# A table-lookup and interaction kernel: the first table's ids sent to all partitions by DMA, the selection columns read with a step of zero

## What is computed

```python
e = jnp.stack([tbl_0[ids[:, 0]], tbl_1[ids[:, 1]], ..., tbl_26[ids[:, 26]]], axis=1)   # (512, 27, 128)
z = dot products of all pairs of rows of one sample, the lower triangle                # (512, 351)
h = jnp.concatenate([z, dense_ctx], axis=1)
h = jnp.maximum(h @ W_top1 + b_top1, 0.0)
h = jnp.maximum(h @ W_top2 + b_top2, 0.0)
y = h @ W_top3
```

## Time and profile before

| what | value |
|---|---|
| median of 3 runs | 109.08 us (108.71 to 110.86) |
| span of the profiled execution | 123.6 us |
| TensorE busy | 106.3 us, 86% |
| VectorE busy | 70.0 us, 57% |
| ScalarE busy | 67.2 us, 54% |
| GpSimd busy | 68.1 us, 55% |
| moved from memory | 12.06 MB, of it 7.75 MB in table and weight loads, 4.07 MB in gathers |
| chain that ended last | TensorE 68%, VectorE 16%, issue 13%, ScalarE 1% |

### The profile page before, as it was taken

How to read it: one execution, slowest core, us unless ns; L and a number is a source line. 1 busy time by engine, 2 the same in 40 slices (tenths; PEclk the granted TensorE clock), 3 DMA queues, 4 the chain that set the end, 5 groups by cost and what they waited for, 6 DMA issues and landing times.

```text
span 123.6 us, 3473 instructions
## 1 busy us (share of the span) xinstructions
PE 106.3 (86%) x1496; PEld 86.1 (70%) x1496; DVE 70.0 (57%) x98; ACT 67.2 (54%) x112; POOL 68.1 (55%) x71
## 2 busy tenths in 40 slices
PE   6998799899999899999329993789458999997992
PEld 6534487687887687788219883669448999797891
DVE  6799999999999999999900050015001060103401
ACT  4596929899999999995200052025301144531442
POOL 3777888888888888887744166416560665000000
PEclk9999999999999999999985599558975699999999
DMA  3896366966984574711210101110200011000000
GB/s 79 262 237 190 101 204 146 293 198 155 302 235 111 172 229 108 205 48 42 54 52 17 31 29 42 27 48 21 66 24 27 21 48 41 23 5 5 5 0 1
DMA packets 5305, 12.06 MB, mean 98 GB/s; under 512 B 1765, under 2 KB 2277, under 8 KB 5290
## 3 DMA queue, kind: packets, MB, share of 16 engines
q1 hardware_dynamic: 3282, 7.75, 22.0%
q0 software_dynamic: 1984, 4.07, 12.8%
q10 hardware_dynamic: 24, 0.02, 0.1%
HBM read 11.83 MB, written 0.00 MB: 96 GB/s over the span
## 4 chain that ended last, share of the span: by engine, by line
PE 68%; DVE 16%; issue 13%; ACT 1%; DVEq 0%
PE ring L512 21%; PE gram_ps L539 12%; DVE marks L651 10%; PE gram_ps L512 8%; PE ring L592 5%; PE ids_ps L574 4%; PE ring L523 4%; DVE low L628 3%; PE ids_ps L567 2%; PE ids_ps L523 2%; PE ring L574 2%; PE ring L602 2%; PE ids_ps L592 1%; DVE pick L610 1%; PE ids_ps L553 1%
## 5 line engine op out<-in xcount | busy, mean ns | idle before, releaser
L422 POOL DMA_INDIRECT rows<-tbl,ids_sb x62 | 67.1, 1082 | 36.3 <-issue 15.9
L651 DVE TENSOR_TENSOR marks<-ids_ps,row_no 125x1024 fp32r<-125x1024 f32 (+2 forms) x39 | 43.5, 1148 | 0.0
L512 PE MATMUL ring<-marks,high 125*128 125x512 f32 (+1 forms) x64 | 26.6, 416 | 1.7 <-issue 1.6
L539 PE MATMUL gram_ps<-rowsT 128*27 128x27 f32 x1024 | 15.8, 206 | 11.4 <-issue 11.2
L512 PE MATMUL ring<-marks,low 125*128 125x512 f32 (+1 forms) x64 | 25.2, 394 | 0.0
L539 PEld LDWEIGHTS gram_ps<-rowsT 128*27 128x27 f32 x1024 | 13.3, 118 | 14.7 <-issue 14.0
L512 PEld LDWEIGHTS ring<-marks,high 125*128 125x128 f32 x64 | 12.8, 200 | 7.1 <-issue 4.6
L724 ACT ACTIVATE away<-ids_ps,row_no 125x512 f32<-125x512 f32 (+1 forms) x22 | 14.0, 715 | 4.7 <-PE ids_ps L466 4.1
L628 DVE TENSOR_TENSOR low<-raw,high 125x512 fp32r<-125x512 f32 (+1 forms) x23 | 16.2, 705 | 0.0
L672 DVE STREAM_TRANSPOSE gram<-gram_ps 128x416 f32<-128x416 f32 (+1 forms) x8 | 4.6, 612 | 18.1 <-PE gram_ps L539 18.1
L512 PEld LDWEIGHTS ring<-marks,low 125*128 125x128 f32 x64 | 12.9, 202 | 1.6
(11 more groups left out here) (61 smaller groups left out, 116.5 us busy)
## 6 DMA issues: line engine op xcount, KB each, us to landing
raw<-tbl SPq DMA_DIRECT2D x9, 448.0 KB
raw<-tbl SPq DMA_DIRECT2D x2, 560.0 KB
rows<-tbl,ids_sb POOLq DMA_INDIRECT x62
w_sb<-w SPq DMA_DIRECT2D x2, 256.0 KB
w_sb<-w SPq DMA_DIRECT2D x1, 512.0 KB
raw<-tbl SPq DMA_DIRECT2D x9, 52.0 KB
raw<-tbl SPq DMA_DIRECT2D x2, 224.0 KB
w_sb<-w SPq DMA_DIRECT2D x1, 192.0 KB
```

The source lines that it names most:

```text
L422: nc.gpsimd.indirect_dma_start(out=rows[0:n, i % ROW_BUFS, s, :], out_offset=None, in_=tables[PLACES[s]], in_offset=bass.IndirectOffsetOnA ...
L512: last = nc.tensor.matmul(bank[:, 0:n], part[:, i % SPLIT_BUFS, c * D:(c + 1) * D], mark_of(unit, c), start=c == 0 and part is high, stop= ...
L539: last = nc.tensor.matmul(gram_ps[s * STRIP:s * STRIP + F, g, 0:F], places, places, start=True, stop=True)
L651: nc.vector.tensor_tensor(marks_of(unit)[:, c0 - c1:, :], index.to_broadcast([TP, c1 - c0, n]), which.to_broadcast([TP, c1 - c0, n]), ALU. ...
```

## The change

The ids of job 0 no longer come over TensorE. A DMA on ScalarE's queue writes them to a new tile `first_ids` on all 128 partitions (the same 2 KB row read 128 times), and VectorE compares them there, still as integers, with a compare of one tensor against a per-partition scalar, 512 marks at a time: eight instructions for the four units. The cast of all ids to floats moves behind the first unit. TensorE's first three spreads are those of jobs 1, 2 and 3 instead of 0, 1 and 2, and there is none left in `find 0 1`. `pick` shrinks to one column per job, the first twelve columns of the identity, and the spread reads that column 128 times with a step of zero, so the two copies that wrote the blocks are gone. ScalarE makes `high` of job 1 ahead of its mark of job 1 instead of behind the distances of job 2.

```diff
-        pick = sb("pick", [P, len(FOUND), P], F32R)
+        pick = sb("pick", [P, len(FOUND)], F32R)
+        first_ids = sb("first_ids", [P, B], I32)
...
             def spread_ids(j):
                 b0, n = JOBS[j]
-                if j >= IDS_BANKS:
+                if j - IDS_BANKS >= 1:
                     pe.wait_ge(marked, through(BY_DVE, j - IDS_BANKS))
-                if j - IDS_BANKS >= 1:
                     pe.wait_ge(away_ready, j - IDS_BANKS)
-                if j == IDS_BANKS:
-                    pe.wait_ge(pick_ready, 2)
-                nc.tensor.matmul(ids_ps[:, j % IDS_BANKS, 0:n], pick[:, j, :], fids_r[:, b0:b0 + n],
+                nc.tensor.matmul(ids_ps[:, j % IDS_BANKS, 0:n], pick[:, j:j + 1].to_broadcast([P, P]), fids_r[:, b0:b0 + n],
                                  start=True, stop=True).then_inc(spread, 1)
...
-            for j in range(IDS_BANKS):
+            for j in range(1, IDS_BANKS + 1):
                 spread_ids(j)
...
-                        if c1 == CHUNKS[i] and i + IDS_BANKS < len(JOBS):
+                        if c1 == CHUNKS[i] and i >= 1 and i + IDS_BANKS < len(JOBS):
                             spread_ids(i + IDS_BANKS)
...
             dve.wait_ge(ident_ready, 1)
-            pick_for(0, IDS_BANKS)
-            dve.wait_ge(fids_cleared, 1)
-            dve.wait_ge(fids_in, 16)
-            nc.vector.tensor_copy(fids_r[0:len(FOUND), :], fids[:, :]).then_inc(fids_ready, 1)
+            nc.vector.tensor_copy(pick[:, :], ident[:, 0:len(FOUND)]).then_inc(pick_ready, 1)
...
+            def ids_ready():
+                dve.wait_ge(fids_cleared, 1)
+                dve.wait_ge(fids_in, 16)
+                nc.vector.tensor_copy(fids_r[0:len(FOUND), :], fids[:, :]).then_inc(fids_ready, 1)
...
-                if c0 == 0:
-                    dve.wait_ge(spread, j + 1)
-                    if j >= 1:
-                        dve.wait_ge(away_ready, j)
+                if u == 0:
+                    dve.wait_ge(first_ids_in, 16)
+                elif c0 == 0:
+                    dve.wait_ge(spread, j)
+                    dve.wait_ge(away_ready, j)
...
+                if j == 0:
+                    for c in range(c0, c1):
+                        last = nc.vector.tensor_scalar(mark_of(unit, c), first_ids[0:TP, 0:n],
+                                                       row_no[CHUNKS[j]][0:TP, c:c + 1], None, ALU.is_equal)
+                        if c == 0:
+                            last.then_inc(first_marked, 1)
+                    last.then_inc(marked, 1)
+                    if c0 == HALF[0]:
+                        subtract(0, 1)
+                    if u == 0:
+                        ids_ready()
+                    return
...
-                if u == 1:
-                    pick_for(IDS_BANKS, len(FOUND))
...
+            nc.scalar.dma_start(first_ids[:, :], found_ids[0:1, :].to_broadcast([P, B])).then_inc(first_ids_in, 16)
             nc.scalar.dma_start(fids[:, :], found_ids).then_inc(fids_in, 16)
...
+            split(1)
             mark(BY_ACT[0])
             distances(BY_ACT[1])
```

More of the change, by code:

```diff
@@ L282, in build @@
         fids_in = sem("fids_in")
+        first_ids_in = sem("first_ids_in")
         first_half_in = [sem(f"first_half_in{h}") for h in range(2)]
@@ L607, in _ @@
         def _(dve):
-            def pick_for(j0, j1):
-                nc.vector.tensor_copy(pick[:, j0:j1, :], ident[:, j0:j1].rearrange("p (k o) -> p k o", o=1)
-                                      .to_broadcast([P, j1 - j0, P])).then_inc(pick_ready, 1)
             nc.vector.memset(gram_ps[:, :, :], 0.0).then_inc(gram_cleared, 1)
@@ L652, in mark @@
                                         which.to_broadcast([TP, c1 - c0, n]), ALU.is_equal).then_inc(marked, 1)
-                if c0 in (0, HALF[j]) and (j, c0) != (0, 0):
+                if c0 in (0, HALF[j]):
                     subtract(j, int(c0 != 0))
-                if u == 1:
-                    pick_for(IDS_BANKS, len(FOUND))
             for step, units in zip(STEPS, marks_order()):
@@ L718, in distances @@
                     act.wait_ge(row_no_ready, len(row_no))
-                act.wait_ge(spread, j + 1)
+                act.wait_ge(spread, j)
                 if j - AWAY_BUFS >= 1:
@@ L750, in _ @@
                 for unit in units:
-                    if unit[1] == 0 and unit[0] + 1 < SPLIT_BUFS:
+                    if unit[1] == 0 and 2 <= unit[0] + 1 < SPLIT_BUFS:
                         split(unit[0] + 1)
```

## The result

| | before | changed |
|---|---|---|
| median | 109.05 us (108.71 to 110.86, 6 runs) | 113.46 us (112.42 to 115.36, 6 runs) |
| ratio changed / before | | 1.035, 95% interval 1.030 to 1.040 |
| span of the profiled execution | 123.6 us, and 106.9 in the second one below | 112.0 us |
| busy: TensorE, VectorE, ScalarE, GpSimd | see the table ahead of the prediction | 99.1, 67.0, 67.3, 68.9 us |

The forecast was 107.4 with a range up to 109.4, so it was wrong, in sign and in size.

What follows compares the result with a forecast made beforehand. VectorE was taken to bound the kernel until about 57 us, TensorE behind that. Table 1 beginning at 9.0 instead of 10.67 us gains 1.7, so the median goes from 109.08 to 107.4 us, range 105.9 to 109.4.

Steps and rivals of the forecast that it cites:

- What bounds the kernel now: Whole kernel: VectorE's pace, 4.60 us per table, sets the time until about 57 us; behind that TensorE is the chain.
- The gathers that follow in the second part: Gathers behind the finding stage: held by counts that TensorE's progress raises, so they move with it; no separate cost given.
- The landing A: Program start: when table 0's ids land on all partitions; taken as 3.8 us, between 3.3 and 5.8.
- a break-even at 5.5: Late landing of table 0's ids: each microsecond costs one, no gain left at A = 5.5 us; chance 0.08.
- The path from A to table 1: VectorE's start: from the ids' landing to the first comparison of table 1, A + 5.2 = 9.0 us.
- The new wait for `high`: VectorE ahead of its first `low`: waits about 1.5 us for ScalarE's copy, paid in full.
- The compare's pitch: VectorE's eight SBUF compares: 0.33 us each, like the cast; the rival of 0.60 had chance 0.08.
- A few tenths more for it cost nothing: GpSimd's gathers, one each 1.25 us: the stage's transposes nowhere wait for rows, so a small delay is free.
- Rival 2: VectorE's compares and GpSimd block each other: compares wait up to 0.95 us each, giving 110.3 to about 115; chance 0.06.
- TensorE's clock: First table matmuls: clock may rise only at about 9 us, losing 1.2 us, still inside TensorE's 1.5 us to spare.
- The step of zero: TensorE's spreads: reading one column with a step of zero costs nothing; if it doubled them, 0.6 us reaches the end.

Runs made afterwards that it cites:

- the second one below: The unchanged kernel before, profiled again for an execution without the long gaps of L539; profiled span 106.9 us.
- the exchanged kernel: Changed kernel with the two id loads on ScalarE's queue in the other order, fids first and the 256 KB behind; 110.48 us, ratio 1.015.
- the kernel with the small dose: Kernel before with one more GpSimd wait ahead of its first gather, for the first spread; 109.91 us, ratio 1.002.

## Why the prediction was wrong, and where it was right

**What bounds the kernel now.** Right up to 57 us. VectorE's laps stay at 4.60 (`low` at 14.83 and 19.43), and what it gains before them it gains at 57 (1.44 us in the kernel with only the small `pick`). *Wrong* was the step to the rest. "The gathers that follow in the second part are held by counts that TensorE's progress raises, so they move with it" was true of the profiled execution only. I had noticed that it was 14.5 us longer than the timed ones, and removed the gaps from the time but not from the argument: with them gone, TensorE comes sooner to the rows, and what had ample room has one microsecond.

**The landing A.** Taken as 3.8 us, between 3.3 and 5.8; measured 5.4 (4.6 us from issue to landing; 4.3 to 5.3 in the four other kernels that have the load). This is a mis-sized term, and it alone takes all of the gain: by the prediction's rule a break-even at 5.5. I leant to the rate of the large table loads; the load behaved nearer to the slow end.

**The path from A to table 1.** Right: A + 5.2 forecast, 10.83 − 5.4 = 5.4 measured. The new wait for `high` came (1.17 us, forecast 1.5). The compare's pitch is 0.41 us (6.61 to 8.26 for four), neither the cast's 0.33, which I had taken for it since types, length and memories are the same, nor the PSUM comparison's 0.60.

**"A few tenths more for it cost nothing"**, said of GpSimd. This step failed, and it is the 4 us. Two causes were in reach. `ids_sb` and the new load are issued at the same time, which the prediction itself says, using it to time the new load from the old one and never the old one under the new: 1.9 us became 4.8, and the first gather went from 2.93 to 5.84. And the compares hold the running gather, 1.24 us more. Together 2.91 + 1.24 = 4.15.

**Rival 2**, compares and GpSimd in each other's way, was the right mechanism in the wrong direction. I priced VectorE waiting; no compare was held noticeably (the first pair of the exchanged kernel is 0.1 us longer), and the gather waited. In three of the four traces with long gathers, the stretched one was that which began inside the first pair of compares; in the fourth it began inside the run of four.

**TensorE's clock.** Right for the start: 0.85 us between weight loads of L507 until 10.7, full rate from there, hidden. Not foreseen: waits of 0.97 and 2.03 us between 70 and 75 us are followed by the lower of the two clocks, worth 1.6 us in the profile.

**The step of zero** costs nothing, as forecast.

How much of the 4.4 us is clock can be bounded from the timed executions, each of which has its mean granted clock on record. Of 44 executions of the kernel before that were timed beside the experiments, 34 had 1.00 (108.67 to 110.18 us), nine 0.984 (110.28 to 111.66) and one 0.752 (123.61). Of the six of the changed kernel one had 1.00 (112.42), four 0.985 (112.80 to 114.18) and one 0.97 (115.36). At an equal clock the change thus costs about 3.2 us at 1.00 (a single execution) and 2.3 at the lower value; the rest of the 4.4 is that the fall comes in five executions of six instead of ten in 44. Such falls also occur without a wait for rows: in the profiled execution of the kernel with the small dose, a slower one (110.86), the clock is at 0.51 from 80 to 82 us, after a gap of 1.35 us.

## What to carry to other kernels

When an engine off the chain issues a stream of work back to back, count its room at each place where the stream is met, in an execution as long as the timed ones, before calling a delay of it free. A load added to the start of a program must be priced for what it does to the small loads issued beside it, not only for its own landing: issued 0.64 us later, in the kernel before, the same 256 KB cost nothing. And when a step is moved away from the first place where a stream is met, look for the next one: here 2.03 us of waiting went, and the stream was on the chain again at its last gather.

## What the runs showed of the hardware

- A 2 KB row written to 128 partitions by one DMA (256 KB): 4.3 to 5.3 us from issue to landing in five kernels.
- A load of 31 KB lands 1.9 to 2.0 us after issue with that load issued 0.64 us behind it or not at all, and 4.5 and 4.8 us in the two kernels that issue it at the same time. Why the step is so sharp stays open; I did not separate queue, engines and memory.
- A gather of 0.94 us is stretched to 2.31 to 2.54 by compares from SBUF to SBUF in four traces, and ends 0.12 us after them in three, 0.82 in one. Compares are hardly delayed.
- Behind 3 us of waiting for rows, 4.39 us of matmuls ran at a granted clock of 0.63, for work that takes 2.77 at 1.00.
- Every profile has gaps in the dot products (L539 and its like) in which TensorE waits for nothing that is shown, the longest 1.0 to 1.8 us and in ten of the eleven later profiles ahead of the last 33 to 35 dot products of `gram 2 0` to `gram 2 2`; eight have another ahead of `turn 2 2`; in the first profile there were 17 at L539, together 11.2 us. What makes them was not found.
